# Loads, tail order, one merged score product, fillers and the first tiles rearranged in a four-layer attention and experts kernel

## The reference, cut to what matters

```python
x = x + tanh(g_xattn[0]) * attention(layernorm(x), ctx)      # 32 heads of 8, rope, causal mask given as a tensor,
                                                             # plus a gated second softmax over the 64 context rows
x = x + tanh(g_ffn[0])   * experts_top1(layernorm(x))        # 8 experts 256x256, softmax gate
x = x + tanh(g_xattn[1]) * wkv(layernorm(x), ctx)            # a recurrence over 64 steps
x = x + tanh(g_ffn[1])   * experts_top2(layernorm(x))        # 8 experts, 704 wide, silu gate, integer softmax router
```

## Time and profile before

| what | us |
|---|---|
| median of 3 runs | 556.06 (555.04 to 563.01) |
| the profiled execution, its own time | 559.51 |
| span of its trace, first to last instruction | 557.5 |
| TensorE busy in the span | 490.0 (88%) |
| VectorE busy | 389.6 (70%) |
| mean granted TensorE clock | 0.936 of full |

### The profile page before, as it was taken

One profiled execution on the slowest core, in us unless ns is written; L12 is line 12 of the kernel. 1 busy time (PEld: TensorE's weight loads), 2 busy tenths in 40 slices (PEclk: granted clock), 3 DMA queues, 4 the chain that ended last, 5 costly groups with the idle time before them and its releaser, 6 DMA issues. The chain is left out here.

```text
span 557.5 us, 10446 instructions
## 1 busy us (share of the span) xinstructions
PE 490.0 (88%) x3147; PEld 362.9 (65%) x3148; DVE 389.6 (70%) x1025; ACT 268.6 (48%) x570; POOL 170.2 (31%) x228
## 2 busy tenths in 40 slices
PE   1587989899899899999998978977889999999994
PEld 0264857757668577577576754644568888788882
DVE  6445378889788888797896786876577666666640
ACT  1536446365274373463561235342365676666651
POOL 3051110411314114114122104221245565655622
PEclk9957999999999997997997796999799999999998
DMA  8800000000000000000000038954466677767721
GB/s 218 245 1 6 2 4 3 1 16 12 1 25 1 2 21 0 5 19 0 16 11 0 25 152 320 354 176 129 173 227 171 225 235 236 208 203 221 232 29 19
DMA packets 20945, 54.98 MB, mean 99 GB/s; under 512 B 5832, under 2 KB 15568, under 8 KB 17968
## 3 DMA queue, kind: packets, MB, share of 16 engines
q1 hardware_dynamic: 15632, 47.99, 25.1%
q0 software_dynamic: 4416, 6.03, 6.1%
q10 hardware_dynamic: 864, 0.54, 0.3%
HBM read 48.79 MB, written 5.24 MB: 97 GB/s over the span
## 5 line engine op out<-in xcount | busy, mean ns | idle before, releaser
L1841 PE MATMUL bank_o<-w,hT 128*128 (+1 forms) x276 | 68.2, 389 | 1.8 <-DVE hT L1292 0.7
L473 POOL TENSOR_SCALAR rstd<-mv 128x1 f32<-128x1 f32 x32 | 7.2, 225 | 187.9 <-DVE mv L930 187.9
L996 DVE TENSOR_REDUCE mx<-bank_s 128x8 f32<-128x512 f32 x64 | 43.6, 688 | 25.7 <-PE bank_s L1592 24.2
L1306 DVE TENSOR_TENSOR wl<-lw,wh 128x1024 fp32r<-128x1024 f32 (+1 forms) x54 | 60.9, 1128 | 0.2 <-ACT wh L601 0.2
L1841 PEld LDWEIGHTS bank_o<-w,hT 128*128 128x128 f32 (+1 forms) x276 | 48.8, 189 | 15.1 <-issue 10.1
L601 ACT ACTIVATE wh<-lw 128x1024 fp32r<-128x1024 f32 (+1 forms) x54 | 52.9, 980 | 0.0
L1590 PE MATMUL bank_s<-Kh,Qx 128*128 128x128 f32 x256 | 47.2, 313 | 5.7 <-ACT Qx L640 5.7
L1590 PEld LDWEIGHTS bank_s<-Kh,Qx 128*128 128x128 f32 x256 | 41.3, 223 | 8.5 <-issue 6.6
L640 ACT ACTIVATE Qx<-qs,CN 128x512 fp32r<-128x512 f32 x64 | 40.1, 710 | 5.2 <-DVE qs L975 5.2
L555 POOL DMA_INDIRECT out_x<-ys,idx_out x18 | 29.0, 1609 | 35.1 <-ACT ys L832 34.3
L1299 DVE TENSOR_TENSOR hh<-sg,bank_s 128x256 f32<-128x256 f32 x46 | 19.2, 417 | 26.9 <-ACT sg L821 26.8
(11 more groups left out here) (336 smaller groups left out, 1172.0 us busy)
## 6 DMA issues: line engine op xcount, KB each, us to landing
lw<-in_w SPq DMA_DIRECT2D x18, 1408.0 KB
up<-in_w SPq DMA_DIRECT2D x5, 1408.0 KB, 6.3
w<-in_w SPq DMA_DIRECT2D x4, 1536.0 KB, 12.1
CT<-in_ctxT SPq DMA_DIRECT2D x1, 1024.0 KB, 10.4
Pt<-in_WT SPq DMA_DIRECT2D x1, 1024.0 KB
mrow<-mhl SPq DMA_DIRECT2D x64, 8.0 KB, 1.9
X<-in_x SPq DMA_DIRECT2D x1, 896.0 KB, 7.0
out_x<-X SPq DMA_DIRECT2D x6, 128.0 KB, 1.7
```

The lines of the kernel that those rows point to most:

```text
L996: dve.tensor_reduce(mx[:, b, :, g, :].rearrange("p s n -> p n s"), bs[n % 2][:, :].rearrange("p (n s k) -> p n s k", n=NP, s=2), AX.X, ALU ...
L1306: dve.tensor_tensor(wl[par][:, :, at:at + k], lw[par][:, :, at:at + k], wh[par][:, :, at:at + k].bitcast(F32), ALU.subtract).then_inc(w_lo, 1)
L1841: ins = pe.matmul(bo[:, 0:HID], hT[0:k, i, :], w2[0:k, bass.ts(e, 1), i, :].rearrange("p o n -> p (o n)"), start=(i == 0), stop=(i == IT - 1))
```

## The change

- Loads: the constants are loaded in two parts (columns up to C_ONE first), the context and the mask in two parts (what tile 0 needs first), each group on a semaphore of its own; Wkv comes after tile 0's context and mask; the first experts' weights are awaited piece by piece; small weights come last.
- Queries: `project_q` reads a copy `HS` of the turned norm with both batches side by side: 2 products with 128 weight columns in place of 4 with 64. ScalarE makes one more copy a tile (`evac_hn`).
- Merged product: `Q2` takes `mrow`'s place. Its partitions 0 to 63 hold the high part of Q, copied from `Qx` by two DMAs of 512 KB a tile (`high_rows`), partitions 64 to 67 the negated maxima. `Kl`'s upper 64 partitions hold the constant that `Lm` held. One product `Kl` by `Q2` stands for the low K product and the shift: three products of 512 columns a bank in place of four. The maxima rows are ordered so that two DMAs, one after the high part and one after the low part, do what eight did.
- Fillers: `fill` (3 products of 512 columns into bank_t1 ahead of `turn_heads`, 2 into bank_b after `turn_k`, for tiles with a `prev`) and `warm` (at the start); their results are not used.
- First tiles: the zero fill of `Q2` comes ahead of the first `rstd_of`; Vx1 and others are zeroed after the first norm; the norm of tile 1 is computed among the maxima of tile 0; `spread` of tiles 0 and 1 is shared, four heads on ScalarE and four on VectorE; K of batch 0 is turned and copied ahead of the rest; the copies into `Kl`'s upper half and the bf16 constants come after the low parts.
- Tail: another order on PE, ACT and DVE. Gate logits of the last tile are ahead of the first early slot; the recurrence's arguments of the last tile are clamped on VectorE instead of ScalarE; both router logits of the last tiles come ahead of slot 3; `gates(3, 1)` and `gates(3, 2)` come ahead of and inside `ranks`, ahead of `rows_of`.

```diff
-            sp.dma_start(CN[:, :], A["const"]).then_inc(ld_const, 16)
-            for name, dst in (("Wq", wq), ("Wkv", wkv)):
-                sp.dma_start(dst[:, :, :], A[name].rearrange("(c p) n -> p c n", p=P)).then_inc(ld_proj, 16)
-            sp.dma_start(CT[:, :, :], ctxT).then_inc(ld_proj, 16)
+            sp.dma_start(CN[:, 0:C_ONE], A["const"][:, 0:C_ONE]).then_inc(ld_const, 16)
+            sp.dma_start(wq[:, :, :], A["Wq"].rearrange("(c p) n -> p c n", p=P)).then_inc(ld_q, 16)
+            sp.dma_start(CT[:, :, 0:P], ctxT[:, :, 0:P]).then_inc(ld_own, 16)
             for half in range(2):
-                sp.dma_start(MK[half * S:(half + 1) * S, :, :], mask_rows).then_inc(ld_attn, 16)
+                sp.dma_start(MK[half * S:(half + 1) * S, 0:BT, :], mask_rows[:, 0:BT, :]).then_inc(ld_own, 16)
+            sp.dma_start(wkv[:, :, :], A["Wkv"].rearrange("(c p) n -> p c n", p=P)).then_inc(ld_kv, 16)
...
             def shift_rows(t):
-                after(sp, m_lo, t, 1, 1)
+                after(sp, m_hi, t, 1, 1)
                 after(sp, t_mm, t - 1, 8, 8)
+                for hl in range(2):
+                    if hl == 1:
+                        after(sp, m_lo, t, 1, 1)
+                    sp.dma_start(Q2[S + 2 * hl:S + 2 * hl + 2, :, :]..., mhl[:, hl, :]...).then_inc(m_row, 16)
...
+            def high_rows(t, par):
+                after(sp, qx, t, HG, HG)
+                after(sp, t_mm, t - 1, 8, 8)
+                for b in range(BT):
+                    sp.dma_start(Q2[0:S, b, :]..., Qx[par][0:S, :, b, :, :]...).then_inc(m_row, 16)
...
+            pool.memset(Q2[:, :, :].bitcast(F32), 0.0).then_inc(filled, 1)
             rstd_of(0, 0)
-            pool.memset(mrow[:, :, :].bitcast(F32), 0.0).then_inc(mrow_zero, 1)
...
             def project_q(t):
-                for b in range(BT):
-                    for c in range(KT):
-                        ins = pe.matmul(bb[b * S:(b + 1) * S, 0:HID], HC[:, c, b, 0:S], wq[:, c, :], ...)
+                for c in range(KT):
+                    ins = pe.matmul(bb[:, 0:HID], HS[:, c, :], wq[:, c, :], ...)
...
-                pe.matmul(o[:, :], Kl[par][:, b, g, :], q, start=True, stop=False)
-                pe.matmul(o[:, :], Kh[par][:, b, g, :], q, start=False, stop=False)
+                pe.matmul(o[:, :], Kh[par][:, b, g, :], q, start=True, stop=False)
                 pe.matmul(o[:, :], mk2[par][:, b, :], Idup[:, 0:S]..., start=False, stop=False)
-            def shift(t, par, g, b):
+            def low_and_shift(t, par, g, b):
                 if g == 0:
-                    after(pe, m_row, t, BT * 64, BT * 64)
-                pe.matmul(o[:, :], Lm[:, :], mrow[:, b, g * 512:(g + 1) * 512], start=False, stop=True).then_inc(t_mm, 1)
+                    after(pe, k_lo, t, BT, BT)
+                    after(pe, m_row, t, 64, 64)
+                pe.matmul(o[:, :], Kl[par][:, b, g, :], Q2[:, b, g * 512:(g + 1) * 512], start=False, stop=True).then_inc(t_mm, 1)
...
+            def fill(o, n):
+                for i in range(n):
+                    pe.matmul(o[:, :], Idup[:, :], w0h[:, 0, 0:2, :]..., start=True, stop=True)
...
+            rotate_q(0)
+            rotate_k(0, 0)
+            low_q(0)
+            rotate_k(0, 1)
+            spread(0, 0, range(HG // 2, HG))
+            mask_low(0, 0)
+            low_k(0, 0)
...
+            for i in range(2):
+                dve.tensor_copy(Kl[i][S:P, :, :, :]..., CN[S:P, C_ONE:C_ONE + P]...).then_inc(prep, 1)
...
+            ln_stats(0, 1)
+            maxima(0, range(1))
+            ln_apply(0, 1)
+            maxima(0, range(1, 2))
...
+            gates(3, 0)
             select(T1, NT)
+            gates(3, 1)
             h_turned(2)
-            ranks()
-            gates(3, 0)
+            ranks(lambda: gates(3, 2))
             rows_of()
-            gates(3, 1)
-            gates(3, 2)
             h_turned(3)
+            gates(4, 0)
             tables()
-            gates(4, 0)
...
-            router_logits(u - 1, bt[1])
             after(pe, x3_in, u, 1, 1)
             turn_h4(u, u % 2, bt[0])
+            router_logits(u - 1, bt[1])
+            router_logits(u, bt[0], h2T)
+            early_up(3, 0)
+            early_up(3, 1)
             turn_h(2)
-            router_logits(u, bt[0])
-            early_up(3, 1)
             late_ranks()
```

More of the change, by code:

```diff
@@ L115, in build @@
         idx_out = keep("idx_out", [P, 1], I32)
-        ys = [keep(f"ys{i}", [P, HID]) for i in range(2)]
+        ys = [keep("ys0", [P, HID])]
         X = keep("X", [P, NT, HID])
@@ L397, in _, with expert_weights @@
-            for c, e, n, raw in w0_raw:
-                sp.dma_start(raw, A["WT"][e:e + n, c * P:(c + 1) * P, :].rearrange("e p n -> p e n")).then_inc(ld_ffn, 16)
-            sp.wait_ge(mrow_zero, 1)
+            def expert_weights(i):
+                c, e, n, raw = w0_raw[i]
+                sp.dma_start(raw, A["WT"][e:e + n, c * P:(c + 1) * P, :].rearrange("e p n -> p e n")).then_inc(ld_w0[min(i, 1)], 16)
+            expert_weights(0)
+            for half in range(2):
+                sp.dma_start(MK[half * S:(half + 1) * S, BT:B, :], mask_rows[:, BT:B, :]).then_inc(ld_far, 16)
@@ L610, in evac_hn @@
                 after(act, hnT, t, 1, 1)
+                after(act, q_mm, t - 1, 1, 1)
+                copy(HS[:, :, :], ba[:, 0:KT * P].rearrange("p (c n) -> p c n", c=KT)).then_inc(hc_self, 1)
                 after(act, kv_mm, t - 1, BT, BT)
@@ L740, in _ @@
             act.wait_ge(zeroed, 10)
-            for b in range(BT):
-                evac_v(0, 0, b)
+            evac_v(0, 0, 0)
             evac_qT(0)
-            evac_kT(0, 0)
+            evac_v(0, 0, 1)
+            evac_kT(0, 0, range(1))
             act.wait_ge(ld_const, 16)
-            spread(0, 0)
-            high_w0()
+            spread(0, 0, range(HG // 2))
+            evac_kT(0, 0, range(1, BT))
+            high_w0(range(1))
             def tile(t, par, prev2, prev, nxt):
@@ L752, in tile @@
                     evac_q(t + 1)
+                if not prev:
+                    high_w0(range(1, 3))
                 if prev:
@@ L767, in tile @@
                 if nxt:
-                    spread(t + 1, 1 - par)
+                    spread(t + 1, 1 - par, range(HG if prev else HG // 2))
                 if not prev:
@@ L976, in low_q, with spread @@
                                   qs[S:P, :, :, :].bitcast(F32), ALU.subtract).then_inc(q_lo, 1)
+            def spread(t, par, heads):
+                after(dve, q_lo, t, 1, 1)
+                for h in heads:
+                    dve.tensor_scalar(Qx[par][:, :, :, h, :], qs[:, :, :, :].bitcast(F32), CN[:, C_HM + h:C_HM + h + 1], None,
+                                      ALU.mult).then_inc(qx, 1)
             def low_k(t, par):
@@ L1236, in early_weights_in, with ranks @@
                 dve.tensor_tensor(tb1[:, :], tw1[:, :], w3[:, 2, :], ALU.add).then_inc(wts1_in, 1)
-            def ranks():
+            def ranks(between):
                 dve.wait_ge(rk_mm, 1)
@@ L1379, in tile @@
                     low_q(t + 1)
+                if nxt and not prev:
+                    spread(t + 1, 1 - par, range(HG // 2, HG))
                 if prev:
@@ L1535, in project_q @@
             def project_q(t):
-                after(pe, hc_self, t, 1, 1)
+                after(pe, hc_self, t, 2, 1)
                 after(pe, q_lo, t - 1, 1, 1)
-                for b in range(BT):
-                    for c in range(KT):
-                        ins = pe.matmul(bb[b * S:(b + 1) * S, 0:HID], HC[:, c, b, 0:S], wq[:, c, :], start=(c == 0), stop=(c == KT - 1))
+                for c in range(KT):
+                    ins = pe.matmul(bb[:, 0:HID], HS[:, c, :], wq[:, c, :], start=(c == 0), stop=(c == KT - 1))
                 ins.then_inc(q_mm, 1)
@@ L1559, in turn_q, with warm, turn_k @@
                 ins.then_inc(qT, 1)
-            def turn_k(t):
+            def warm(n):
+                for i in range(n):
+                    pe.matmul(bt[1][:, 0:HID], ident, wq[:, 0, :], start=True, stop=True)
+            def turn_k(t, first=False):
                 for b in range(BT):
+                    if first and b == 1:
+                        warm(1)
                     after(pe, k_rot, t, BT, b + 1)
@@ L1650, in values @@
                 ins.then_inc(pv_mm, 1)
+            def fill(o, n):
+                for i in range(n):
+                    pe.matmul(o[:, :], Idup[:, :], w0h[:, 0, 0:2, :].rearrange("p e n -> p (e n)"), start=True, stop=True)
             def turn_heads(t, following, o=bc):
@@ L1869, in tile @@
                 if prev:
+                    fill(bt[1], 3)
                     turn_heads(t - 1, True)
```

287 lines of the change are left out of this document (151 added, 136 removed).

## The result

The changed kernel took 545.95 us in the median of 4 runs (539.96 to 549.62) beside 559.48 for the kernel before: ratio 0.9707 [0.9640, 0.9774]. In a later set of 6 runs it took 542.07 beside 556.80, ratio 0.9729 [0.9662, 0.9796]. The ratios leave out runs that took over 1.5% more than the fastest of their kernel, which the medians count. The profiled execution of the first set took 543.49 us, with a span of 541.6 and a mean granted clock of 0.954 (before: 559.51, 557.5 and 0.936). So 15.9 us of span went, where I had forecast 24.

A forecast was written before the change was run, and what follows sets the result against it. It took TensorE to bound the regular slots, TensorE and VectorE the tiles, a chain the start. Terms -9, -1, -2.5, -2.5, -1, -8 sum to -24 from 559.5 us: 535.5 profiled, 535 on the median's scale; range 523 to 549.

The forecast's parts named there:

- Start: Everything up to tile 0's first low-and-shift product: from 53.1 to near 44 us, -9 us; -5 to -14 possible.
- the step that gave 3.7 us back: In the start, VectorE's list ahead of the first maximum: 6 us, giving back 3.7 of 7.8 us won at row scores.
- Tile 0: Halved `spread` of tile 1 leaves the path to the first exponential, with 8 products less: -1 us, between 0 and -3.
- Tiles 1 to 6: Eight products less and five fillers more a tile: -0.4 us a tile, -2.5 us in all, between -11 and +7.
- the clock in them: Fillers in the tiles' thinnest stretch win back part of some 6.5 us lost at low clock: -2.5 us, between +6 and -6.5.
- Tile 7 and tail: Tile 7: fewer products, no copy of eight, -1 us. Tail: new order from rank products to table and before, -8 us.
- The other swaps -1: In the tail, the reorderings besides the gates and the router logits: -1 us of the tail's -8.
- (a): Rival: the clock holds from the start on, in start, tiles and tail; 524 us, chance 0.15.
- (d): Rival: copies of the high rows are slow, each us over 25 costing seven tiles; 570 us at 30, chance 0.04.
- (b): Rival: the fillers lift nothing, the rest holds; 538 us, chance 0.11 together with (e).
- (e): Rival: the merge fails to make TensorE lighter in the tiles, four records remain; 538 us, chance 0.11 together with (b).
- (c): Rival: waits move on, start -5, tiles 0, tail -3; 551 us profiled, 548 on the median's scale, chance 0.16.

The follow-up runs named there:

- e1: The changed kernel run again unaltered, in the later set of 6 runs: median 542.07 us, ratio 0.9729 to the kernel before.
- e8: The kernel before with only the tiles' filler products added: median 555.58 us, ratio 0.9929 to the kernel before.
- e9: The changed kernel, fillers kept, with the high K product issued twice so each bank has four products: median 544.08 us, ratio 0.9730 to the kernel before.
- e7: The changed kernel with `select` ahead of `gates(3, 0)` and `turn_y(u)` behind `early_up(2, 2)`: median 538.93 us, ratio 0.9622 to the kernel before.
- e4: The changed kernel with the old tail order on three engines, up to the regular slots: median 547.69 us, ratio 0.9817 to the kernel before.
- e5: The changed kernel with loads issued in the old order, each consumer on its own semaphore: median 548.00 us, ratio 0.9803 to the kernel before.

## Why the prediction was right, and where not

The time (545.95 against 535) lies in the range, 523 to 549, and on the forecast side, but outside the inner band, 528 to 544, and the terms were off in both directions. That the sum came this near is in part luck: the start gave 4 us more than its term and the tail 8 us less. The forecast stands for 535.5 us of a profiled execution, which took 543.49.

- Start, forecast -9: measured -13.3, and -13.7 in e1 (-11.9 against e8, whose trace has the old start too). The mechanism was as described, for zero fill, loads and spread alike. Mis-sized was the step that gave 3.7 us back: VectorE's list between row scores and third unit took 4.1 us (20.65 to 24.79), not 6. Its spreads take 0.42 each, not ScalarE's 0.62, and the constant copies 0.65, not 1.2. From the third unit to the turned maxima it was 10.0, not 13; I had left the clock at 0.51 there and it was 0.70. What I had set at 3.5 after the maxima took 5.1: VectorE's query rotation took 1.83 us beside GpSimd's `w0l`, and TensorE waited 1.85 us for what comes of it (38.60 above).
- Tile 0, -1: measured -0.5 in the first trace, +0.8 in e1. Right, and nothing.
- Tiles 1 to 6, -2.5, and the clock in them, -2.5: together -4.7, right as a sum and wrong in its parts. "What remains is attend 3", -0.4 a tile from the merge, was nothing: at full clock tile 5 takes 37.7 us with four products (e9) or three (e1) and tile 3 with four (before), with VectorE as the engine that doesn't get lighter. Tile 1 even lost 1.2 us by the low clock that came with the merge. The clock term was 6 us for the fillers alone, of which 1.4 only made good what the merge had lost. The rule of the Trainium skill (TensorE: Matmul & The Clock Gate, Part 1) that I set beside it, by which the fillers take all 6.5 us, was nearer to the fillers' 6 us than the -2.5 I took; the tiles as a whole, -4.7, were nearer to my -5.
- Tile 7 and tail, -1 and -8: measured from tile 7's landmark to the end, +0.1 in e1 and +2.6 in the first trace, of which the low clock at 372 to 376 us and a regular loop 1.8 us longer (148.9 and 147.1) are part. This is the step that failed: "both router logits ahead of slot 3 bring the ranks forward, -1.5". The ranks came 4.8 us later in e1, because `select` stands behind `gates(3, 0)` in VectorE's list (3.1 us by e7) and because in TensorE's list eight products of slot 3 and `turn_h(2)` now stand between the last router products and the ranks, where there were four products. "The other swaps -1" is in the same loss: `turn_y(u)` ahead of `early_up(2, 2)` waited 1.97 us in e1. The logits themselves came no earlier: counted from tile 7 the last router products start at 63.4 us in e1 and at 63.5 in e4, and the ranks 7.7 us behind them in place of 3.4. I had taken the place of the logits in their own list for their time, and had not followed the list of the engine that reads them. The other half, -5.5 from ranks to table, was measured at -5.7 in e1 and -4.0 in the first trace.
- Rivals: (a) didn't come, the clock was 0.77 from 24 to 46 us and not full. (d) never showed, no copy of the high rows ended a wait of a merged product. (b) and (e) were half true, the merge did nothing and the fillers much. (c), waits that move on, is what happened in the tail alone. The point that the loop would be "as long as before" held to 0.2 us in e1 (146.9 us from the second late rows to the end, 147.1 before).

## What to carry to other kernels

When steps are reordered, follow each moved result into the list of its reader: a result that is early is worth nothing behind an instruction that waits for something late, and here the new order of the lists took back 4.2 of the 5.7 us that a closed hole gave (e1 beside e4). When an engine isn't the bound, taking work off it is not free: here its clock fell with its load, and a few products without use put into its idle places were worth 6 us, where the product saved was worth nothing that the traces show. Compare variants by a landmark for each stage and at equal clock; medians alone would have put 5 us on a tail order that is worth 0.6.

## What the runs showed of the hardware

- The clock column doesn't show the first slow stretch. In the timeline of the changed kernel the four value products at 9.52 us take 3.78 us and the next four of the same shape, at 13.84, take 1.88, while the granted clock reads 1.00 over both. The trace's first record of the clock stands at 13.7 us, and the column reads 1.00 ahead of it. In e1 and e5 that record stands at 11.1 and 18.6 us, and there too the four products ahead of or across it take longer (2.79 and 3.67 us) than the four behind it (1.88 in both). The timeline's rows and, behind them, the windows':

```profile
9.52 3.78 PE L1596 MATMUL bank_c<-wkv,HC 128*128 128x512 f32 x4
...
13.84 1.88 PE L1596 MATMUL bank_a<-wkv,HC 128*128 128x512 f32 x4
```

```profile
9.00:13.00 4.00, 4.00 (x6) 1.41 (x5) 1.57 (x5) 0.38 (x1) 0.00 (x0) 1.00 1.05 354
13.00:16.00 3.00, 3.00 (x14) 1.89 (x13) 2.12 (x5) 1.89 (x5) 0.00 (x0) 1.00 1.20 275
```

- GpSimd slows VectorE with a plain zero fill (0.41 to 3.59 us), and with a subtraction too: the 256-element rotation product, 0.41 us in a regular tile, took 1.83 while GpSimd's ran, which reaches to 37.14.

```profile
34.79 2.35 POOL L510 TENSOR_TENSOR w0l<-VE,w0h 128x1024 fp32r<-128x1024 f32 x1
35.59 1.83 DVE L980 TENSOR_TENSOR qt<-qw,CN 128x256 f32<-128x256 f32 x1
```

- The same program meets different amounts of low clock from run to run: spans of 539.2 to 540.2 us at 0.953 and of 547.0 and 547.7 at 0.938. What decides between them stays open.
